# Transposing the query and key stacks by DMA instead of on TensorE

## The reference

```python
h = einsum('bhid,oi,od->bho', x, weighted_sum, weight)        # token mixing
h = h + attention(layernorm(h), qkv_w, qkv_b, out_w, out_b)   # 16 heads of 16
h = h + moe_ffn(layernorm(h), Wg, bg, W1, b1, W2, b2)         # 8 experts, hidden 1024
```

## Time and profile before

| | |
|---|---|
| median of 3 runs | 2082.81 us (2080.15 to 2085.11) |
| span of the profiled execution | 2077.0 us |
| PE busy | 1927.9 us (93%) |
| ACT busy | 1142.8 us (55%) |
| DVE busy | 823.0 us (40%) |
| POOL busy | 675.0 us (33%) |
| DMA moved | 176.92 MB, 23.6% of 16 queues' time |

### The profile page before, as it was taken

The page is one execution under the profiler, slowest core; times in us unless marked ns, Lnnn a source line. Parts: engine busy times, 40 slices in busy tenths (PEclk is TensorE's granted clock), DMA queues, the critical chain, the costliest instruction groups (busy, mean ns, idle before and its releaser), DMA issues.

```text
span 2077.0 us, 36719 instructions
## 1 busy us (share of the span) xinstructions
PE 1927.9 (93%) x13152; PEld 1212.8 (58%) x13152; DVE 823.0 (40%) x1716; ACT 1142.8 (55%) x1969; POOL 675.0 (33%) x570
## 2 busy tenths in 40 slices
PE   5679798898999989999999989999899998999998
PEld 4246544676556764567546765467645675466665
DVE  5656833547104560146313371144711464032111
ACT  2654667444764466544775448644576446654443
POOL 1112422334323342334323243233423333234443
PEclk8789999999999999999999999999999999999999
DMA  4113322421213221231122221123112311122221
GB/s 150 48 51 105 125 99 102 158 97 62 82 62 104 91 73 65 88 113 62 62 80 86 91 81 62 62 104 111 61 62 86 114 68 70 62 82 92 102 85 48
DMA packets 40461, 176.92 MB, mean 85 GB/s; under 512 B 4056, under 2 KB 17120, under 8 KB 23904
## 3 DMA queue, kind: packets, MB, share of 16 engines
q1 hardware_dynamic: 40288, 174.52, 23.6%
HBM read 153.54 MB, written 20.97 MB: 84 GB/s over the span
## 4 chain that ended last, share of the span: by engine, by line
PE 75%; DVE 11%; issue 5%; ACT 2%; POOL 1%; DVEq 0%; ACTq 0%; POOLq 0%
PE bank_h L862 26%; PE bank_f L881 11%; PE bank_f L884 10%; PE bank_f L883 10%; PE bank_o L791 5%; PE bank_s L779 3%; PE bank_s L695 2%; PE bank_s L697 2%; PE bank_s L696 2%; DVE gs L1082 1%; DVE acc L1086 1%; DVE tmp_b L977 1%; DVE y L900 1%; PE bank_s L764 1%; PE bank_s L845 1%
## 5 line engine op out<-in xcount | busy, mean ns | idle before, releaser
L550 POOL TENSOR_TENSOR hl<-h,hh 128x512 f16<-128x512 f32 x512 | 606.0, 1184 | 1198.2 <-ACT hh L672 749.9
L862 PE MATMUL bank_h<-x,w1s 128*128 128x512 f16 x3072 | 761.1, 385 | 20.3 <-issue 9.9
L669 ACT ACTIVATE h<-bank_h,b1s 128x512 f32<-128x512 f32 x512 | 352.3, 688 | 493.6 <-PE bank_h L862 479.6
L881 PE MATMUL bank_f<-w2s,hh 128*128 128x256 f16 x2048 | 568.4, 278 | 44.0 <-DVE acc L1086 43.1
L883 PE MATMUL bank_f<-w2s,hh 128*128 128x256 f16 x2048 | 566.3, 277 | 0.0
L884 PE MATMUL bank_f<-w2s,hl 128*128 128x256 f16 x2048 | 566.0, 276 | 0.0
L862 PEld LDWEIGHTS bank_h<-x,w1s 128*128 128x128 f16 x3072 | 289.3, 99 | 350.3 <-issue 56.9
L639 ACT ACTIVATE probs<-bank_s 128x512 f32<-128x512 f32 x480 | 261.6, 601 | 163.4 <-PE bank_s L779 163.3
L672 ACT ACTIVATE hh<-bank_h,b1s 128x512 f16<-128x512 f32 x512 | 351.1, 686 | 0.0
L881 PEld LDWEIGHTS bank_f<-w2s,hh 128*128 128x128 f16 x2048 | 203.4, 99 | 169.5 <-issue 53.5
L883 PEld LDWEIGHTS bank_f<-w2s,hh 128*128 128x128 f16 x2048 | 203.1, 99 | 47.3 <-issue 0.6
(11 more groups left out here) (136 smaller groups left out, 1825.5 us busy)
## 6 DMA issues: line engine op xcount, KB each, us to landing
w1s<-w_parts SPq DMA_DIRECT2D x56, 1024.0 KB, 4.8
w2s<-w_parts SPq DMA_DIRECT2D x56, 1024.0 KB, 4.8
xraw<-in_x_t_dram SPq DMA_DIRECT2D x32, 512.0 KB, 4.2
raw<-in_w_dram SPq DMA_DIRECT2D x16, 1024.0 KB, 6.3
w_parts<-w1s SPq DMA_DIRECT2D x8, 1024.0 KB, 8.8
w_parts<-w2s SPq DMA_DIRECT2D x8, 1024.0 KB, 10.7
out_dram<-acc SPq DMA_DIRECT2D x16, 256.0 KB, 4.6
raw<-in_qkv_w_t_dram SPq DMA_DIRECT2D x1, 768.0 KB, 7.4
```

The lines of the kernel that those rows point to most:

```text
L550: pool.tensor_tensor(hl[n % HBUFS][:], h32[n % 2][:], hh[n % HBUFS][:], ALU.subtract)\
L669: act.activation(h32[n % 2][:], bank_h[n % 2][:, :], ACT.Relu, bias=b1s[:, e, m:m + 1]).then_inc(h_hi.sem, 1)
L862: last = pe.matmul(bank_h[n % 2][:, :], w[:, wp, k, m * P:(m + 1) * P], x16[:, xp, k, :], start=(k == 0 and wp + xp == 0), stop=(k == DK - ...
L881: pe.matmul(o, high, w[:, 0, m, :], start=(m == 0 and t % 2 == 0), stop=False, skip_group_check=True)
```

## The change

`qk_turn` is taken out on PE and on ACT. In its place SP issues a transposing DMA per tile and half, from `stack` in SBUF to `qt` or `kt` in SBUF, once DVE has signalled `stack_ready`. The next tile's `stack` stages on ACT and DVE wait for the landing of these transfers, and so does the first `scores` step of a batch. SP's loop over the batches is written out, and the transposes are placed in SP's program after `load_expert(b, 3)`, for batch 1 around `load_raw(4)`, and for batch 0 before `load_raw(1)`. The fp16 identity and its cast on POOL go away.

```diff
-                  (17.1 + 1.5 * t, "unit", t), (18.6 + 1.5 * t, "stack", t), (20 + 1.5 * t, "qk_turn", t)]
+                  (17.1 + 1.5 * t, "unit", t), (18.6 + 1.5 * t, "stack", t)]
...
+            def turn_stacks(b, tiles):
+                for t in tiles:
+                    for a in range(2):
+                        wait(sp, stack_ready, b, 2 * t + a + 1)
+                        if t == 0:
+                            wait(sp, scored, b, 0)
+                        sp.dma_start_transpose((qt, kt)[a][:, :, t * P:(t + 1) * P],
+                                               stack[:, a].rearrange("p h s d -> p (h s d)"))\
+                          .then_inc(stack_turned[a].sem, 16)
...
             load_x(1, [0, 1])
+            turn_stacks(0, range(TT))
             load_raw(1)
...
             for e in range(2, EXPERTS):
+                if e == 3:
+                    turn_stacks(1, range(TT // 2))
                 if e + 1 < EXPERTS:
                     load_raw(e + 1)
+                if e == 3:
+                    turn_stacks(1, range(TT // 2, TT))
                 store_parts(e)
...
                 for e in range(2, EXPERTS):
                     load_expert(b, e)
+                    if more and e == 3:
+                        turn_stacks(b + 1, range(TT))
...
-            with sp.Fori(1, BATCHES - 2) as i:
+            for i in range(1, BATCHES - 2):
                 body(i, True, True)
...
                 elif stage == "stack":
                     wait(act, qk_unit, ab, n + 1)
                     for a in range(2):
-                        wait(act, stack_turned, ab, 2 * (n - 1) + a + 1)
+                        wait(act, stack_turned[a], ab, 16 * n)
                         high, _, unit_qk = stack_slots(n, a)
                         copy(high, unit_qk).then_inc(stack_hi.sem, 1)
-                        if n:
-                            take_turned(n - 1, a, ab, fb is None)
-                elif stage == "qk_turn" and n == TT - 1:
-                    for a in range(2):
-                        take_turned(n, a, ab, fb is None)
...
-                elif stage == "qk_turn":
-                    ...
-                        for h in range(HEADS // 2):
-                            last = pe.transpose(turned[:, h, :], stack[...], ident16[:])
-                        last.then_inc(stack_turned.sem, 1)
                 elif stage == "scores":
                     if n == 0:
-                        wait(pe, qt_out, ab, TT)
-                        wait(pe, kt_out, ab, TT)
+                        for turned in stack_turned:
+                            wait(pe, turned, ab, 16 * TT)
...
                         wait(dve, stack_hi, ab, 2 * n + a + 1)
-                        wait(dve, stack_turned, ab, 2 * (n - 1) + a + 1)
+                        wait(dve, stack_turned[a], ab, 16 * n)
                         dve.tensor_tensor(low, unit_qk, high, ALU.subtract).then_inc(stack_ready.sem, 1)
```

More of the change, by code:

```diff
@@ L67, in attention_order @@
         order = ["ln1_turn 0", "ln1_turn 1", "qkv 0", "rotate 0", "ln1_turn 2", "qkv 1", "rotate 1", "qk_norm 0",
-                 "unit 0", "ln1_turn 3", "qkv 2", "stack 0", "rotate 2", "unit 1", "qkv 3", "qk_turn 0", "stack 1",
-                 "rotate 3", "qk_norm 1", "qk_turn 1", "unit 2", "stack 2", "unit 3", "qk_turn 2", "stack 3",
-                 "qk_turn 3"]
+                 "unit 0", "ln1_turn 3", "qkv 2", "stack 0", "rotate 2", "unit 1", "qkv 3", "stack 1",
+                 "rotate 3", "qk_norm 1", "unit 2", "stack 2", "unit 3", "stack 3"]
         places = {name: 8 + 0.1 * k for k, name in enumerate(order)}
@@ L217, in build @@
         ident = sb("ident", [P, P])
-        ident16 = sb("ident16", [P, P], F16)
         mix = sb("mix", [P, 2, XK, D], F32R)
@@ L341, in build @@
         stack_ready = signal("stack_ready", 2 * TT)
-        stack_turned = signal("stack_turned", 2 * TT)
-        qt_out = signal("qt_out", TT)
-        kt_out = signal("kt_out", TT)
+        stack_turned = [signal(f"stack_turned{a}", 16 * TT) for a in range(2)]
         scored = signal("scored", 4 * UNITS)
@@ L388, in qkv_banks @@
             return bank_h if alone and t % 2 else bank_s
-        def qk_turn_bank(a, alone):
-            return (bank_f if alone else bank_s)[a][:, :].bitcast(F16).rearrange("p (h t) -> p h t", t=P)
         def stack_slots(t, a):
@@ L575, in _ @@
             pool.wait_ge(consts_in, 16 * 9)
-            pool.tensor_copy(ident16[:], ident[:]).then_inc(pool_consts, 1)
             run(pool, steps)
@@ L582, in copy @@
                 return act.activation(out_ap, in_ap, ACT.Copy)
[L584 to L589, removed]
             def split_x(b, t):
@@ L753, in steps @@
                     last.then_inc(qkv_done.sem, 1)
-                elif stage == "qk_turn":
[L755 to L762, removed]
-                        for h in range(HEADS // 2):
-                            last = pe.transpose(turned[:, h, :],
-                                                stack[:, a, 2 * h:2 * h + 2, :, :].rearrange("p h s d -> p (h s d)"),
-                                                ident16[:])
-                        last.then_inc(stack_turned.sem, 1)
                 elif stage == "scores":
@@ L786, in steps @@
                         wait(pe, ln1_lo, ab, TT)
+                        if fb is None:
+                            pe.wait_ge(pool_consts, 1)
                     if tile == 0:
```

## The result

| | before | after |
|---|---|---|
| median | 2082.1 us (10 runs) | 2093.0 us (10 runs, 2083.3 to 2095.1) |
| ratio | | 1.0051 [1.0035, 1.0067] |
| span of the profiled execution | 2077.0 us | 2093.3 us |
| PE busy | 1927.9 us | 1907.2 us |
| ACT busy | 1142.8 us | 1088.5 us |

The account below looks back on a forecast made before the run. PE was taken as the bound (busy 93%). Six batches at 3.8 us (22.8), batch 0's 4.0 and batch 1's 8.5 gave +35 on 2077.0, 2112, plus 5.8 for the median: 2118 us; range 2060 to 2240, own 2095 to 2170.

Parts of the forecast that it names:

- What left PE: On PE, 4 turns of 0.89 us per batch go, 3.6 us; 21.6 us over batches 2 to 7.
- the costs named as nothing: SP's loop written out, and expert 4's weight load queued behind a batch's transposes, costing only if a transfer exceeded 9 us.
- the price of T: T, from DVE's end of a half to the transfer's landing: taken as 4.6 us, lower end 2.8, upper 8.8.
- The formula: Batch 3's scores can start at 752.0 + four transfers in a row + 3 x 1.4 us: 774.6, before 772.4.
- PE's wait ahead of the scores: Batches 2 to 7: PE idle 5.8 us before each batch's first scores, in one or several pieces.
- What the steady batches lose: Batches 2 to 7: scores 2.2 us later plus 1.6 us of lower clock, 3.8 us per batch, 22.8 in all.
- Batch 0: Nothing runs beside its transfers; first scores at 82.4 against 78.4 us, +4.0 us.
- Batch 1: Tile 2's transfers queue behind load_raw(4); scores at 263.3 against 256.4, +6.9 and 1.6 for the clock: +8.5 us.
- Rival A: Transfers quick enough, 2.8 us each, scores set by PE's own work: sum -14.5, 2068 us; chance 0.22.
- Rival B: Transposing transfers as slow as large stores, 8.8 us, through short pieces or queue waits: sum +152, 2234 us; chance 0.30.
- clock term: After PE's new stall before the scores, the granted clock is lower: 1.6 us lost per batch.
- The signs named: ACT's stack stages idle some 2 us for tile 1, more for 2 and 3; PE idle before scores; clock 0.50 after.

Follow-up runs that it names:

- e7: Changed kernel with two stack buffers, batch 1's tile 2 transfers issued between the halves of load_raw(4), and scores one chunk later: 2064.6 us, ratio 0.9919.
- e10: Kernel before, with PE's turns, given two stack buffers and the scores one chunk later (gates' memory shared to make room): 2084.7 us, ratio 1.0026.
- e4: Kernel before with SP's loop over the batches written out and nothing else: 2082.1 us, ratio 0.9999.
- e6: Changed kernel, still one stack buffer, with the scores and what follows them one chunk later: 2077.2 us, ratio 0.9981.
- e2: Changed kernel with a second stack buffer: 2071.3 us, ratio 0.9962.
- e1: Changed kernel with batch 1's tile 2 transfers issued between the two halves of load_raw(4): 2090.3 us, ratio 1.0041.

## Why the prediction was off

**What left PE** was right: 3.6 us per batch, shown by e7 against e10 as 3.7. So were the costs named as nothing: SP's written-out loop (e4), and the wait of expert 4's weights behind the transposes, of which no trace shows a sign.

**The step that failed is the price of T.** I took 4.6 us, the landing of the output stores, as the nearest row. From issue to landing it is 2.7 to 2.8, and 4.2 to 4.9 in one of eight transfers of most batches. From the end of the low part, the four second halves of a batch have 3.5, 3.5, 4.3 to 5.1 (3.0 in batch 4) and 2.7 (3.2 in batch 4): T is 3.3 to 3.7 on the mean of a batch, under the forecast's own 3.8 to 6.5. With 3.5 the error over four links is 4 x 1.1 = 4.4 us per batch. The row of 2.8 us, set down as the lower end, was the right one for the landing. Why is not shown: that row is a load from DRAM and the output a store to it, and the transfers do neither.

**A second error went the other way.** The formula took all four links as set by T. In batch 4 the first link, from 1004.78 + 1.28 = 1006.1 to 1013.2, is 7.1 us long, where T + 1.4 = 4.9: ACT reached tile 1's stack at 1010.6 by its own list, and no transfer held it. The same could be read before, where that link is 758.5 - 752.0 = 6.5 us. Together: scores 23.9 us after the first low part's start by the formula with T = 4.6, less 4.4, plus 2.2, is 21.7; the mean of batches 2 to 7 is 21.3 and, profiled again, 21.5, where before it is 22.2 and 21.7 (e4). PE's wait ahead of the scores, forecast at 5.8 us, is 2.9.

**What the steady batches lose.** The forecast had 3.8 us each. The period went from 244.6 and 244.8 (e4) to 245.1, 245.5 and 246.5 in three traces with one stack and the scores in their old place: 0.3 to 1.9 us. The terms of the sum were the right ones: in the first pair of traces 3.6 us of turns go, 2.6 us of idle time come, and the lower clock takes 1.4, against 1.6 forecast. That makes up the 0.5 of this pair. Filling PE's wait (e6) or shortening the chain (e2) takes the loss away.

**How much was luck.** With T = 3.5 and nothing else altered, the forecast's own sum is -3.6 for the six batches, +1.8 for batch 0 and +7.4 for batch 1, some +6 us. So the direction did not need the wrong T, but it then hangs on batch 1 and the clock, and the margin is close to what a measurement can tell.

**Batch 0** was 1.1 us later in place of 4.0, with T = 3.5 in 73.2 + 2T = 80.2 against the measured 79.6. **Batch 1**'s scores were 6.4 us late in place of 6.9. That step had its mechanism, the landing behind the raw load (6.4 us for the query half), and about its size: from the batch's first low part it is 31.8 and 31.9 us in two executions against 25.4 and 27.0 before, 4.8 to 6.5 more. Undone, however, it gave back 3 us of time, not 8.5.

**The rivals.** Rival A was nearer with T (a mean of 3.3 to 3.7, against its bound of 3.7) and had the wrong outcome: its sum gives about -5 us at T = 3.5, because it has no clock term for the six batches and takes the first link as set by T. Rival B fell: its short pieces are there (packets under 512 B went from 4056 to 71640), and the transfers still land in 2.7 us. The signs named did appear: ACT idle about 2 us on tile 2, PE idle before the first scores, half the clock after it in four of six batches. Only ACT on tile 1 did not wait.

## What to carry over

When work moves from an engine to a transfer, its busy time goes and its latency comes; with a single buffer the latency counts once per tile, in a chain. Look at each link for what would end it last, the transfer or the engine's own list, and then at what the bound engine has to do meanwhile. Here the change lost 0.5% as made; one more buffer, or a later place of the first consumer, turned it into a gain of 0.4 or 0.2%, and both with batch 1's order into one of 0.8%. Read more than one batch before a wait is given a size: the one shown first here had the shortest.

## What was not expected of the hardware

On the median a DMA transpose costs SP 1.23 to 1.30 us per instruction at 128 x 1024 and 1.27 at 128 x 512, four times the 0.32 of the weight loads in the earlier trace rows; with two per tile the second waits for the first's issue. The landing depends little on the size: 2.7 us for 256 KB, 2.4 for 128 KB. Five of 48 transfers landed in 4.2 to 4.9 us, each with one 16 KB packet of the kind "instruction" inside it. A wait of PE of 1.9 us was followed by a granted clock of 0.56 over the next 3 us; but the length of the wait alone doesn't tell. In three executions (the changed kernel twice, e1) there are 18 such waits of 1.8 to 3.7 us in batches 2 to 7; behind 12 the clock fell, behind 6 it stayed full, one of 3.7 us among them.
